# Three box filters and a Fourier block in one program: VectorE's sums, residuals and root in another order, a root of eleven operations, two mixes swapped, GELU ahead of the square

## The chip, the core and the metric

The program runs on one core of one Trainium2 chip. The metric is the device time of a run in microseconds, the median of the runs; lower is better. Everything is computed in float32.

## The reference, cut to what matters

The input is `x` of shape (4, 64, 128, 128): four images with 64 channels. Four layers follow each other. Layers 0, 2 and 3 are box filters with a batch norm on either side; the change does not touch them. Layer 1 is a stack of four identical blocks, and that is where the change lies:

```python
def _block(x, ...):                       # four times, each with its own weights
    residual = x
    xn = _ln(transpose(x), ln1w, ln1b)    # layer norm over the 64 channels: mean, variance, rsqrt
    xf = rfft2(xn)
    o1 = relu(complex_mix(xf, w1) + b1)   # first mix: 64x64 complex, per frequency
    o2 = complex_mix(o1, w2) + b2         # second mix
    o2 = o2 * mask                        # zero where both |re| and |im| are at most 0.01
    x = residual + irfft2(o2)
    xp2 = _ln(transpose(x), ln2w, ln2b)   # second layer norm
    return x + gelu(xp2 @ mw1 + mb1) @ mw2 + mb2
```

Each layer norm needs, for each pixel, the sum and the sum of squares over the channels and then 1/sqrt(variance + 1e-5). The last is what the text calls the root.

## The kernel before, in words

The four images times four blocks make 16 passes through layer 1 (`RUNS`, numbered n = 0 to 15). The function `afno_layers` writes them as a pipeline by hand: while the MLP of pass n runs over 16 blocks of eight rows, the Fourier part of pass n+1 runs in the same stretch. A pass is cut into 16 periods q = 0 to 15, one for each block of rows, and each period into four steps s = 0 to 3; `parts` says which piece of the Fourier part lies in which step: the second half of the inverse transform of pass n in the periods 0, 1 and 4, the forward transform of n+1 in 4 and 5, the mixes (`spectrum`) from 5 to 10, the backward transform in 11, and the first half of the inverse transform in 12 and 13. Every engine walks through the same loop over n, q and s and issues its own share in the order in which the Python code of that engine stands; semaphores tie the engines together. There is no scheduler: the order of the lines is the order on the engine.

What each engine does in a period, with the lines of the profile:

- **TensorE (PE)** turns the previous delta back (`turn_back`, L1765 into the PSUM tile `result`), turns the next normalised block (`turn`, L1759, from `y2`), multiplies with the MLP's weights (`mlp_up` L1739, `mlp_down` L1750 into `result`), and its part of the Fourier transform (inverse L1667 and L1671, forward L1685, spectrum L1696, L1705 and L1714, backward L1729). `mlp_down(i)` writes the same PSUM tile that the residual of block i-1 is read from, so it waits for that residual.
- **VectorE (DVE)** adds the residual (`residual`, L1433), adds the inverse transform's output (`inverse`, L1371, L1372, L1376), takes the sums for the layer norms (`sum_up`: L1452 for the sum, L1455 for the sum of squares), and runs the root (`root`, lines L986 to L1006): twelve small operations on at most 128 x 64 elements that depend on each other one by one. The root of a set of four blocks starts a chain of POOL's.
- **GpSimd (POOL)** finishes the inverse transform (L1263), folds the rows for the forward transform (`fold`, L1298 and L1300), and multiplies with the root: `normalise` (L1275) makes `y2` for PE's turn, `next_y` (L1287) makes the next pass's rows. The first `normalise` after a root and `next_y` wait for that root; the rest only follow in POOL's order.
- **ScalarE (ACT)** takes the squares (`square`, L1593), the GELU (`gelu`, L1559), the copy of the turned block (L1565), the delta for `turn_back` (`mlp_delta`, L1572) and other evictions.
- **SyncE (SP)** loads and stores rows.

The change edits the loops of VectorE, ScalarE and TensorE at the periods q = 1, 2, 10, 13, 14 and 15, and the function `root_step`. Before, VectorE runs the root of the periods 1 and 2 in one piece at q = 1, s = 2, ahead of that period's inverse; and at q = 13 all four sums of two strips follow the inverse, so the residual of q = 14 stands behind them, and the root behind the residual.

## Time and profile before

| | us |
|---|---|
| Three runs: median (lowest to highest) | 3559.46 (3558.67 to 3560.19) |
| The profiled execution: its own time / its span | 3561.85 / 3560.0 |
| Busy in the span: PE / PE's weight loads / DVE / ACT / POOL | 3248.4 / 1965.7 / 2393.6 / 2205.7 / 1649.7 |
| Mean granted TensorE clock | 0.963 of full |

The profile is that of one execution. Its span runs from the first to the last instruction. A gap in square brackets behind a row of the timeline is the idle time of that engine just before the row, and the name behind the arrow is what ended it. Layer 1 fills the stretch from about 190 us to 3170 us; one undisturbed pass of the pipeline takes 174.5 us of it.

### The profile page before, as it was taken

What the parts mean: (1) busy time and instruction counts of PE and PEld (TensorE: products, weight loads), DVE (VectorE), ACT (ScalarE), POOL (GpSimd) and SP (SyncE); (2) the same over time, 40 slices, a digit from 0 to 9 for tenths busy, and PEclk for the clock granted to TensorE, in tenths of its full rate; (3) what the DMA queues carried; (4) which work ended last, traced back from release to release, by engine and by line L of the source; (5) the groups of instructions that cost most, each with busy time, mean ns of one, the idle gap of its engine ahead of it and who ended that gap; (6) DMA issues with size and microseconds to landing.
All of it is one profiled execution on the core that took longest, in us unless ns stands there. A gap on an engine that the chain in (4) does not pass through costs nothing. (4 is left out here: it accounts for less than half of the span.)

```text
span 3560.0 us, 52776 instructions
## 1 busy us (share of the span) xinstructions
PE 3248.4 (91%) x18285; PEld 1965.7 (55%) x18285; DVE 2393.6 (67%) x4148; ACT 2205.7 (62%) x3477; POOL 1649.7 (46%) x1389
## 2 busy tenths in 40 slices
PE   6946699999999999998999999999999999979689
PEld 2735464647474646464647464646474747334257
DVE  4956666767676676766667667676767665536677
ACT  3954466666666666666666666666656565646468
POOL 4435545464646454545454645455454543210242
PEclk7967899999999999999999999999999999999889
DMA  9850001010101011313120101111111111356898
GB/s 324 275 187 24 30 31 62 34 65 31 66 31 66 31 66 37 118 48 137 48 89 31 66 31 65 37 60 44 57 42 54 42 54 42 147 188 190 262 303 239
DMA packets 250279, 334.08 MB, mean 94 GB/s; under 512 B 22304, under 2 KB 195616, under 8 KB 242608
## 3 DMA queue, kind: packets, MB, share of 16 engines
q1 hardware_dynamic: 241664, 315.29, 26.3%
q0 software_dynamic: 7904, 15.57, 1.6%
q8 instruction: 144, 2.36, 0.3%
q14 instruction: 103, 0.84, 0.1%
q10 hardware_dynamic: 464, 0.02, 0.0%
HBM read 188.06 MB, written 142.74 MB: 93 GB/s over the span
## 5 line engine op out<-in xcount | busy, mean ns | idle before, releaser
L1559 ACT ACTIVATE images<-a_wide,a_up_b 128x1024 f32<-128x1024 f32 x512 | 569.8, 1113 | 247.2 <-PE a_wide L1739 245.8
L1739 PE MATMUL a_wide<-images 64*128 64x512 f32 x2048 | 579.2, 641 | 23.8 <-ACT images L1559 23.1
L1317 POOL TENSOR_TENSOR images<-a_o,a_mag 128x256 f32<-128x256 f32 (+1 forms) x512 | 360.6, 731 | 378.3 <-DVE a_mag L1422 378.3
L1750 PE MATMUL a_result<-images 128*64 128x512 f32 x2048 | 499.0, 607 | 34.8 <-DVE images L1433 34.8
L1275 POOL TENSOR_TENSOR images<-images,a_stat 128x512 f32<-128x512 f32 x256 | 268.6, 1050 | 545.7 <-DVEq L1469 527.0
L1402 DVE TENSOR_TENSOR a_o<-a_bank,a_mix_b 128x512 f32<-128x512 f32 (+1 forms) x272 | 180.9, 665 | 249.6 <-PE a_bank L1714 246.7
L1705 PEld LDWEIGHTS a_bank<-a_dft_h,a_g 128*128 128x128 f32 x2080 | 273.5, 192 | 129.9 <-issue 129.9
L1433 DVE TENSOR_TENSOR images<-a_result,images 128x512 f32<-128x512 f32 x256 | 175.6, 686 | 224.8 <-PE a_result L1765 224.6
L1750 PEld LDWEIGHTS a_result<-images 128*64 128x64 f32 x2048 | 128.6, 136 | 355.6 <-issue 339.9
L1739 PEld LDWEIGHTS a_wide<-images 64*128 64x128 f32 x2048 | 156.7, 185 | 287.8 <-issue 258.0
L1455 DVE TENSOR_REDUCE a_stat<-a_sq 128x16 f32<-128x1024 f32 x240 | 290.7, 1211 | 10.5 <-ACT a_sq L1593 8.6
L1696 PE MATMUL a_bank<-a_xf,a_mix_fold 128*128 128x512 f32 (+1 forms) x544 | 286.4, 608 | 5.8 <-ACT a_xf L1546 5.8
L1685 PE MATMUL a_bank<-dft_w,images 128*128 128x128 f32 x2048 | 246.2, 279 | 48.4 <-POOL images L1300 46.2
L1263 POOL TENSOR_TENSOR images<-images,a_odd 128x512 f32<-128x512 f32 (+1 forms) x128 | 161.6, 1263 | 270.1 <-DVE images L1372 260.8
L1572 ACT ACTIVATE images<-a_result,a_down_b 128x512 f32<-128x512 f32 x256 | 175.8, 687 | 176.6 <-PE a_result L1750 176.1
L1452 DVE TENSOR_REDUCE a_stat<-images 128x16 f32<-128x1024 f32 x232 | 281.5, 1213 | 4.8
L1685 PEld LDWEIGHTS a_bank<-dft_w,images 128*128 128x128 f32 x2048 | 235.4, 193 | 84.2 <-POOL images L1300 46.3
L1705 PE MATMUL a_bank<-a_dft_h,a_g 128*128 128x128 f32 x2080 | 278.3, 276 | 1.8 <-DVE a_g L1395 1.8
L1593 ACT ACTIVATE a_sq<-images 128x1024 f32<-128x1024 f32 x216 | 227.3, 1052 | 68.8 <-DVE a_stat L1455 43.0
L1729 PE MATMUL a_bank<-a_dft_hi,images 128*128 128x128 f32 x2048 | 235.4, 277 | 8.9 <-POOL images L1317 8.9
L1729 PEld LDWEIGHTS a_bank<-a_dft_hi,images 128*128 128x128 f32 x2048 | 232.3, 194 | 12.8 <-POOL images L1317 12.8
L1520 ACT ACTIVATE a_g<-a_bank 64x252 f32<-64x252 f32 (+3 forms) x512 | 166.6, 374 | 77.5 <-PE a_bank L1685 58.2
(206 smaller groups left out, 6119.7 us busy)
## 6 DMA issues: line engine op xcount, KB each, us to landing
rows<-images SPq DMA_DIRECT2D x112, 512.0 KB, 2.6
images<-rows SPq DMA_DIRECT2D x105, 512.0 KB, 3.7
box_xc<-in_x SPq DMA_DIRECT2D x16, 1024.0 KB, 16.7
box_x<-in_x SPq DMA_DIRECT2D x64, 256.0 KB, 4.3
turned<-box_o SPq DMA_DIRECT2D x64, 256.0 KB, 3.6
images<-turned SPq DMA_DIRECT2D x16, 1024.0 KB, 11.8
planes<-box_work SPq DMA_DIRECT2D x64, 256.0 KB, 3.7
box_xc<-planes SPq DMA_DIRECT2D x16, 1024.0 KB, 19.2
```

The costliest lines, as they stand in the source:

```text
L1275: G.tensor_tensor(rows(y2[:, i % 2]), x[:, row:row + HB], r[:, :, None].broadcast_to([P, HB, C]), ALU.mult).then_inc(s_y2, 1)
L1317: ins = G.tensor_tensor(y[n % 2][:, :, to].rearrange("p c k -> p k c"), o2[:, j % 3, lo:4, r], mask[:, lo:4], ALU.mult)
L1452: V.tensor_reduce(to, strip, AX.X, ALU.add)
L1455: V.tensor_reduce(to, squares_of(r, kind, u), AX.X, ALU.add).then_inc(s_sq_read, 1)
L1559: A(hidden[:, i % 2, j], wide[:], ACT.Gelu, bias=up_b2[:, l, j:j + 1]).then_inc(s_hid, 1)
L1593: A(squares_of(r, kind, u), strip, ACT.Square).then_inc(s_sq, 1)
L1685: mm = M(bank[i % 4][:, c * P:(c + 1) * P], y[n % 2][:, 4 * i + c, :], dft_w[:], start=True, stop=True)
L1696: M(bank[2][:, 0:cols], mix1_fold[:, l], xf[:, 0:cols], start=True, stop=True).then_inc(s_mix1, 1)
L1705: mm = M(bank[0][:, k * P:(k + 1) * P], g[:, first_kw(t) + k].rearrange("p r c -> p (r c)"), dft_h[:], start=True, stop=True)
L1729: mm = M(bank[i % 4][:, c * P:(c + 1) * P], y[n % 2][:, 4 * i + c, :], dft_hi[:], start=True, stop=True)
L1739: mm = M(wide[:, half * BANK:(half + 1) * BANK], up_fold[cs, l, j * P:(j + 1) * P], yc[cs, i % 2], start=True, stop=True)
L1750: mm = M(result[half * C:(half + 1) * C, :], down[:, l, j, :], hidden[:, i % 2, j, half * BANK:(half + 1) * BANK], start=j == 0, stop=j == ...
```

## The change

It does five things; no matrix product, sum, residual or DMA is added or taken away.

- The root takes eleven operations: the shift and the subtraction of its first guess become one multiplication and addition.
- At q = 1 VectorE issues the inverse first, then the first five operations of the root; the other six follow the residual at q = 2.
- At q = 13 the sum of the strip of q = 12 goes ahead of the inverse; the sum of squares of the strip of q = 13 moves behind the residual of q = 14, and the one of q = 14 behind the residual of q = 15.
- TensorE issues the last but one second mix ahead of the last first mix.
- ScalarE issues the second GELU of q = 14 ahead of that period's square, and in passes that do not stage a new image also at q = 15.

```diff
-ROOT_STEPS = 12
+ROOT_STEPS = 11
...
-        ins = V.tensor_scalar(r.bitcast(I32), v.bitcast(I32), 1, None, ALU.logical_shift_right)
-    elif j == 4:
-        ins = V.tensor_scalar(r.bitcast(I32), r.bitcast(I32), -1.0, float(RSQRT_GUESS), ALU.mult, ALU.add)
+        ins = V.tensor_scalar(r.bitcast(I32), v.bitcast(I32), -0.5, float(RSQRT_GUESS), ALU.mult, ALU.add)
...
                     if q not in CLOSED and 0 <= Q - 2 < BLOCKS * RUNS:
                         residual(Q - 2)
-                    if q == 14 and FIRST_ROOT <= r < END_ROOT:
-                        root(r, range(ROOT_STEPS))
-                    strips = (strips_at(n, 12)[1:] if q == 13 else []) + strips_at(n, q)[:1]
+                    if q == 2 and FIRST_ROOT <= SETS * n < END_ROOT:
+                        root(SETS * n, range(ROOT_STEPS // 2, ROOT_STEPS))
+                    if q == 13:
+                        for strip in strips_at(n, 12)[1:]:
+                            sum_up(*strip, 0)
+                    if q == 14:
+                        for strip in strips_at(n, 13)[:1]:
+                            sum_up(*strip, 1)
+                        if rooted:
+                            root(r, range(ROOT_STEPS))
+                    if q == 15:
+                        for strip in strips_at(n, 14)[:1]:
+                            sum_up(*strip, 1)
+                    strips = strips_at(n, q)[:1]
...
                         parts(n, q, s, inverse, forward, spectrum, backward)
+                        if q == 13 and s == 1:
+                            for strip in strips_at(n, 12)[1:]:
+                                sum_up(*strip, 1)
                         if s == late:
                             for strip in strips:
                                 sum_up(*strip, 0)
-                                if q not in CLOSED:
+                                if q not in CLOSED and q not in (13, 14):
                                     sum_up(*strip, 1)
...
-                            if q == 1 and s == (2 if q in CLOSED else 1):
-                                root(r, range(ROOT_STEPS))
-                            if (q, s) in ((5, 3), (9, 2)):
+                            if (q, s) in ((1, 3), (5, 3), (9, 2)):
                                 root(r, range(ROOT_STEPS // 2))
...
-                    if q != 12 and not (q % 4 == 3 and fresh(n)):
+                    if q not in (12, 14, 15) and not (q % 4 == 3 and fresh(n)):
                         for strip in strips_at(n, q):
                             square(*strip)
                     parts(n, q, 1, inverse, forward, spectrum, backward)
                     if q not in CLOSED and 0 <= Q < BLOCKS * RUNS:
                         gelu(Q, 1)
-                    if q == 12:
+                    if q in (12, 14) or q == 15 and not fresh(n):
                         for strip in strips_at(n, q)[:1]:
                             square(*strip)
...
+                    if t == N_CHUNK:
+                        second_mix(t - 2)
+                    if 0 <= t - 1 < N_CHUNK:
+                        first_mix(t - 1)
```

On VectorE at the periods 1 and 2 of a pass, before: the end of the root (its last three operations of twelve, L996 to L1006), the inverse of q = 1 (L1371 to L1376), the residual of q = 2 (L1433), then a sum.

```order
L996 TENSOR_TENSOR a_stat<-a_stat 128x64
L1004 SCALAR_TENSOR_TENSOR a_stat<-a_stat 128x64
L1006 SCALAR_TENSOR_TENSOR a_stat<-a_stat 128x64
L1371 TENSOR_TENSOR images<-a_bank,images 128x512
L1372 TENSOR_TENSOR images<-a_bank,images 128x512
L1376 TENSOR_TENSOR images<-a_bank,images 128x512
L1433 TENSOR_TENSOR images<-a_result,images 128x512
L1452 TENSOR_REDUCE a_stat<-images 128x16
```

And with the change (line numbers of the new file: the inverse is L1369 to L1374, the residual L1431, the sums L1450 and L1453):

```order
L1453 TENSOR_REDUCE a_stat<-a_sq 128x16
L1369 TENSOR_TENSOR images<-a_bank,images 128x512
L1370 TENSOR_TENSOR images<-a_bank,images 128x512
L1374 TENSOR_TENSOR images<-a_bank,images 128x512
L986 SCALAR_TENSOR_TENSOR a_stat<-a_stat 128x64
L988 SCALAR_TENSOR_TENSOR a_stat<-a_stat 128x64
L990 TENSOR_SCALAR a_stat<-a_stat 128x64
L992 TENSOR_SCALAR a_stat<-a_stat 128x64
L994 TENSOR_TENSOR a_stat<-a_stat 128x64
L1431 TENSOR_TENSOR images<-a_result,images 128x512
L996 TENSOR_TENSOR a_stat<-a_stat 128x64
L998 SCALAR_TENSOR_TENSOR a_stat<-a_stat 128x64
```

The inverse moved ahead of the whole root, and seven of the root's twelve operations no longer stand ahead of the residual: five do.

On VectorE from the period 13 to the start of the root at 14, before: the residual of q = 13, the inverse, the sums of two strips (`a_mag` holds the squares of the first), the residual of q = 14, the root.

```order
L1433 TENSOR_TENSOR images<-a_result,images 128x512
L1371 TENSOR_TENSOR images<-a_bank,images 128x512
L1372 TENSOR_TENSOR images<-a_bank,images 128x512
L1376 TENSOR_TENSOR images<-a_bank,images 128x512
L1452 TENSOR_REDUCE a_stat<-images 128x16
L1455 TENSOR_REDUCE a_stat<-a_mag 128x16
L1452 TENSOR_REDUCE a_stat<-images 128x16
L1455 TENSOR_REDUCE a_stat<-a_sq 128x16
L1433 TENSOR_TENSOR images<-a_result,images 128x512
L986 SCALAR_TENSOR_TENSOR a_stat<-a_stat 128x64
```

And with the change:

```order
L1431 TENSOR_TENSOR images<-a_result,images 128x512
L1450 TENSOR_REDUCE a_stat<-images 128x16
L1369 TENSOR_TENSOR images<-a_bank,images 128x512
L1370 TENSOR_TENSOR images<-a_bank,images 128x512
L1374 TENSOR_TENSOR images<-a_bank,images 128x512
L1453 TENSOR_REDUCE a_stat<-a_mag 128x16
L1450 TENSOR_REDUCE a_stat<-images 128x16
L1431 TENSOR_TENSOR images<-a_result,images 128x512
L1453 TENSOR_REDUCE a_stat<-a_sq 128x16
L986 SCALAR_TENSOR_TENSOR a_stat<-a_stat 128x64
```

Two of the four sums no longer stand between the inverse and the residual of q = 14: one went ahead of the inverse, one behind the residual.

On TensorE at the period 10, before: the last first mix (L1696), the last but one second mix (L1714 from `a_odd`), the turns, the last second mix (L1714 from `a_o`).

```order
L1739 MATMUL a_wide<-images 128x512 x2
L1696 MATMUL a_bank<-a_xf,a_mix_fold 128x512
L1714 MATMUL a_bank<-a_mix,a_odd 128x128 x4
L1765 MATMUL a_result<-ident,images 128x128 x4
L1759 MATMUL a_turned<-ident,images 128x128 x4
L1714 MATMUL a_bank<-a_mix,a_o 128x128 x4
```

And with the change (L1757, L1783 and L1777 are the old L1739, L1765 and L1759; the first mix is L1707):

```order
L1757 MATMUL a_wide<-images 128x512 x2
L1714 MATMUL a_bank<-a_mix,a_odd 128x128 x4
L1707 MATMUL a_bank<-a_xf,a_mix_fold 128x512
L1783 MATMUL a_result<-ident,images 128x128 x4
L1777 MATMUL a_turned<-ident,images 128x128 x4
L1714 MATMUL a_bank<-a_mix,a_o 128x128 x4
```

The second mix went ahead of the first mix; nothing else moved there.

## Rows read from the trace of the kernel before

**Rows 1.** Stretches: us, busy PE, PEld, DVE, ACT, POOL, PEclk, DMA, GB/s.
```profile
2183.30:2357.80 174.50, 169.62 (x974) 102.84 (x972) 122.14 (x215) 110.15 (x163) 91.19 (x77) 1.00 0.14 49
...
1851.20:1854.60 3.40, 3.40 (x10) 1.06 (x8) 1.74 (x2) 1.34 (x2) 3.40 (x3) 0.50 0.02 5
```

**Rows 2.** Groups of PE by line, whole span: busy, mean ns | idle before.
```profile
L1750 PE MATMUL a_result<-images 128*64 128x512 f32 x2048 | 499.0, 607 | 34.8 <-DVE images L1433 34.8
...
L1759 PE MATMUL a_turned<-ident,images 128*128 128x128 f32 x1024 | 156.2, 275 | 32.3 <-POOL images L1275 32.3
```

**Rows 3.** Timeline of PE, pass 10, periods 14 and 15: start, us.
```profile
2345.31 0.66 PE L1765 MATMUL a_result<-ident,images 128*128 128x128 f32 x4
...
2348.70 1.94 PE L1750 MATMUL a_result<-images 128*64 128x512 f32 x8 [0.88 <-DVE images L1433]
...
2352.68 0.66 PE L1759 MATMUL a_turned<-ident,images 128*128 128x128 f32 x4 [0.40 <-POOL images L1275]
...
2354.68 1.94 PE L1750 MATMUL a_result<-images 128*64 128x512 f32 x8 [0.29 <-DVE images L1433]
2356.78 1.13 PE L1739 MATMUL a_wide<-images 64*128 64x512 f32 x4 [0.16 <-ACT images L1559]
```

**Rows 4.** Timeline of PE, pass 10, periods 2 to 4.
```profile
2200.20 1.94 PE L1750 MATMUL a_result<-images 128*64 128x512 f32 x8 [0.93 <-DVE images L1433]
...
2204.50 1.13 PE L1739 MATMUL a_wide<-images 64*128 64x512 f32 x4 [0.28 <-ACT images L1559]
2205.56 1.94 PE L1750 MATMUL a_result<-images 128*64 128x512 f32 x8
...
2210.24 0.66 PE L1759 MATMUL a_turned<-ident,images 128*128 128x128 f32 x4 [1.10 <-POOL images L1275]
```

**Rows 5.** Timeline of PE, pass 10, period 11.
```profile
2309.58 0.60 PE L1729 MATMUL a_bank<-a_dft_hi,images 128*128 128x128 f32 x3 [0.28 <-POOL images L1317]
```

**Rows 6.** Timeline of DVE, pass 10, periods 13 and 14.
```profile
2341.43 0.69 DVE L1371 TENSOR_TENSOR images<-a_bank,images 128x512 f32<-128x512 f32 x1 [1.09 <-PE a_bank L1671]
...
2345.62 1.21 DVE L1452 TENSOR_REDUCE a_stat<-images 128x16 f32<-128x1024 f32 x1
...
2347.87 0.68 DVE L1433 TENSOR_TENSOR images<-a_result,images 128x512 f32<-128x512 f32 x1
2348.47 0.22 DVE L986 SCALAR_TENSOR_TENSOR a_stat<-a_stat 128x64 f32<-128x64 f32 x1
```

**Rows 7.** Timeline of POOL, pass 10, period 14.
```profile
2351.59 1.04 POOL L1275 TENSOR_TENSOR images<-images,a_stat 128x512 f32<-128x512 f32 x1 [7.44 <-DVEq L1469]
```

**Rows 8.** Timeline of ACT, pass 10, period 15.
```profile
2354.57 1.06 ACT L1593 ACTIVATE a_sq<-images 128x1024 f32<-128x1024 f32 x1 [0.60 <-DVE images L1433]
```

**Rows 9.** Timeline of DVE, pass 10, periods 1 and 2.
```profile
2193.99 0.54 DVE L986 SCALAR_TENSOR_TENSOR a_stat<-a_stat 128x64 f32<-128x64 f32 x1
...
2197.44 0.69 DVE L1371 TENSOR_TENSOR images<-a_bank,images 128x512 f32<-128x512 f32 x1
...
2199.37 0.68 DVE L1433 TENSOR_TENSOR images<-a_result,images 128x512 f32<-128x512 f32 x1
```

**Rows 10.** Timeline of POOL, pass 10, periods 1 and 2.
```profile
2198.88 1.27 POOL L1263 TENSOR_TENSOR images<-images,a_odd 128x512 f32<-128x512 f32 x1 [4.42 <-DVE images L1372]
2200.10 2.40 POOL L1300 TENSOR_TENSOR images<-images,a_upper 128x1024 f32<-128x1024 f32 x1
2202.44 1.06 POOL L1275 TENSOR_TENSOR images<-images,a_stat 128x512 f32<-128x512 f32 x1
```

**Rows 11.** Timeline of DVE in the start-up: a root beside folds.
```profile
252.71 2.23 DVE L990 TENSOR_SCALAR a_stat<-a_stat 128x32 f32<-128x32 f32 x1
254.97 2.24 DVE L992 TENSOR_SCALAR a_stat<-a_stat 128x32 int32<-128x32 int32 x1
```

**Rows 12.** Timeline of POOL in the same stretch: the second of two folds.
```profile
254.85 2.32 POOL L1300 TENSOR_TENSOR images<-images,a_upper 128x960 f32<-128x960 f32 x1
```

**Rows 13.** Timeline of PE, pass 8, period 2.
```profile
1850.83 3.38 PE L1750 MATMUL a_result<-images 128*64 128x512 f32 x8 [1.97 <-DVE images L1433]
```

More of the change, by code:

```diff
@@ L991, in root_step @@
     elif j == 3:
-        ins = V.tensor_scalar(r.bitcast(I32), v.bitcast(I32), 1, None, ALU.logical_shift_right)
-    elif j == 4:
-        ins = V.tensor_scalar(r.bitcast(I32), r.bitcast(I32), -1.0, float(RSQRT_GUESS), ALU.mult, ALU.add)
-    elif j in (5, 9):
+        ins = V.tensor_scalar(r.bitcast(I32), v.bitcast(I32), -0.5, float(RSQRT_GUESS), ALU.mult, ALU.add)
+    elif j in (4, 8):
         ins = V.tensor_tensor(total, r, r, ALU.mult)
+    elif j == 5:
+        ins = V.tensor_tensor(total, total, v, ALU.mult)
     elif j == 6:
-        ins = V.tensor_tensor(total, total, v, ALU.mult)
+        ins = V.scalar_tensor_tensor(out=total, in0=total, scalar=-10.0 / 3.0, in1=total, op0=ALU.add, op1=ALU.mult)
     elif j == 7:
-        ins = V.scalar_tensor_tensor(out=total, in0=total, scalar=-10.0 / 3.0, in1=total, op0=ALU.add, op1=ALU.mult)
-    elif j == 8:
         ins = V.scalar_tensor_tensor(out=r, in0=total, scalar=5.0, in1=r, op0=ALU.add, op1=ALU.mult)
-    elif j == 10:
+    elif j == 9:
         ins = V.scalar_tensor_tensor(out=total, in0=total, scalar=-0.5 * CUBIC ** 3, in1=v, op0=ALU.mult, op1=ALU.mult)
@@ L1476, in _ @@
                         fold_weights()
+                    rooted = FIRST_ROOT <= r < END_ROOT
                     if q in CLOSED and 0 <= Q - 2 < BLOCKS * RUNS:
@@ L1696, in spectrum, with second_mix @@
                         M(bank[2][:, 0:cols], mix1_fold[:, l], xf[:, 0:cols], start=True, stop=True).then_inc(s_mix1, 1)
+                    def second_mix(j):
+                        pe.wait_ge(s_o1, before + j + 1)
+                        if j >= 1:
+                            pe.wait_ge(s_o2, before + j)
+                        for k in range(chunk(j)):
+                            mm = M(bank[3][:, k * P:(k + 1) * P], o1_of(j)[:, k * P:(k + 1) * P], mix2[:, l],
+                                   start=True, stop=True)
+                        mm.then_inc(s_mix2, 1)
+                    if t == N_CHUNK:
+                        second_mix(t - 2)
+                    if 0 <= t - 1 < N_CHUNK:
+                        first_mix(t - 1)
                     if t < N_CHUNK:
@@ L1707, in spectrum @@
                         mm.then_inc(s_fh, 1)
-                    j = t - 2
-                    if 0 <= j < N_CHUNK:
-                        pe.wait_ge(s_o1, before + j + 1)
-                        if j >= 1:
-                            pe.wait_ge(s_o2, before + j)
-                        for k in range(chunk(j)):
-                            mm = M(bank[3][:, k * P:(k + 1) * P], o1_of(j)[:, k * P:(k + 1) * P], mix2[:, l],
-                                   start=True, stop=True)
-                        mm.then_inc(s_mix2, 1)
+                    if t >= 2 and t != N_CHUNK:
+                        second_mix(t - 2)
                     if t == 8:
```

5 lines of the change are left out of this document (2 added, 3 removed).

## The prediction

> **What bounds the kernel now.** I read the stretches first, then PE's groups by line, then the timelines of PE, VectorE, POOL and ScalarE in one pass. In pass 10 PE is busy 169.6 of 174.5 us at the full clock [rows 1]; the other engines are at most 70% busy. So PE's work sets the length of a pass, and an edit on another engine gains only what it takes out of PE's waits. Two of those waits are large in the groups by line: `mlp_down` (L1750) waits 34.8 us for the residual, and the turn (L1759) waits 32.3 us for POOL's multiplication by the root [rows 2]. Both come once per pass at fixed places, so I work in pass 10 and multiply. Its waits are, at q = 14 and 15: 0.88 for the residual, 0.40 for POOL, 0.29 for the residual, 0.16 for the GELU [rows 3]; at q = 2: 0.93 for the residual; at q = 4: 1.10 for POOL [rows 4]; at q = 11: 0.28 for POOL's masked product [rows 5]. Together 4.04 us. A shown gap understates its wait a little: L1750 follows L1739 after 1.06 us where nothing waits, although L1739 lasts 1.13 [rows 4]; so 0.07 more goes with each, 4.5 us in all. Over 15 passes that is an upper limit of about 68 us.
>
> **Periods 13 to 15.** Before, VectorE is free for the third of four sums at 2345.62, runs two more to 2347.87 and only then adds the residual [rows 6], whose input PE had ready at 2345.31 + 0.66 = 2345.97 [rows 3]. With the change two sums stand there instead of four. The one put ahead of the inverse takes (2347.87 - 2345.62) / 2 = 1.13 us and falls into the 1.09 us in which VectorE waits for PE anyway [rows 6], so it costs nothing; without that cover it would cost 1.13 us of VectorE's time, and the residual would still come 0.7 us earlier. The residual starts at about 2346.0, 1.85 us earlier, and PE's wait of 0.88 + 0.07 = **0.95** goes. The root follows: residual 0.6, one sum 1.13, a handover of 0.1 give 2347.85 instead of 2348.47; from there to POOL's L1275 it is 2351.59 - 2348.47 = 3.12 us for twelve operations [rows 6, 7], 0.26 each, and eleven save 0.26. So POOL starts 0.6 + 0.2 = 0.8 us earlier. PE, 0.95 earlier, waits for it a little longer than before, and what is left is 0.8. At q = 15 the residual no longer stands behind a sum of squares: 0.29 + 0.07 goes. ScalarE's square of 1.06 us [rows 8] now follows the GELU, so the GELU that PE waits for comes earlier, and 0.16 + 0.07 goes. The square then delays the delta that the next turn back needs; by my count it ends 0.05 to 0.1 us before PE wants it, so this term is full or lost by a tenth. Sum for q = 13 to 15: **-1.4 us** a pass.
>
> **Periods 1 to 4.** This is the disputed part. Before, the root runs from 2193.99 to the inverse at 2197.44, and the residual follows at 2199.37, 1.93 us for three additions [rows 9]. During the root POOL sits idle: its L1263 waits 4.42 us for the inverse's second addition and starts at 2198.88, then the fold L1300 and L1275 follow without a gap [rows 10]. With the change the inverse comes first, 2193.99 to 2195.9, and POOL starts as much ahead of the additions' end as before, 2199.37 - 2198.88 = 0.49, so at 2195.4; the fold runs from 2195.4 + 1.22 = 2196.6 to 2199.0. Now the first five operations of the root run beside L1263 and the fold. What that costs is seen in the start-up: an operation of the root that takes 0.18 to 0.26 us alone took 2.23 and 2.24 us beside POOL's fold [rows 11]; the second was issued at 254.97, just behind the start of a fold at 254.85, and ended when that fold did [rows 12]. So one operation of the root gets in between two POOL instructions, and the next waits for the whole of the second. The Trainium skill (SBUF — State Buffer, Who interferes with whom) says the same: one port pair is shared by VectorE and GpSimd and held for a whole instruction, by VectorE when both its inputs lie in SBUF or it runs in a two-port mode, never by a reduction. By that rule, taken strictly with the fold already queued, the very first operation would wait for the fold's end too, and a pass would gain 0.25 us less; the rows show one getting through, and I keep to them.
>
> So L986 ends with L1263 at 2196.6, L988 with the fold at 2199.0, and three more take 0.75: the residual comes at 2199.75, **0.38 later** than before although seven operations of the root moved behind it. PE's wait at q = 2 grows by 0.38. Without the block it would come at 2195.9 + 5 x 0.26 = 2197.2, two us earlier than before, and the wait of 1.0 would go; these are the ends of this term, and the rows on the block are nearest. The second half, six operations of 0.26 behind a residual of 0.6, with POOL idle and waiting for them, ends at 2201.9, and L1275 starts at 2202.0 instead of 2202.44. From there to the turn at q = 4 POOL runs without a gap, so the turn comes 0.44 earlier, which leaves PE **-0.45 us** over the stretch, the 0.38 included.
>
> **Period 10.** The swapped mixes and the shorter first half of that root let VectorE's last masks come 0.2 to 0.5 us earlier, and with them the masked product that PE waits for at q = 11. Between 0 and 0.28 + 0.07, and a tenth at the mix itself, I take **-0.4**. The first mix, 0.9 later, feeds ScalarE just in time.
>
> **Sum.** A pass gains 1.4 + 0.45 + 0.4 = 2.25 us. That holds for eleven passes, 0 to 5 and 9 to 13: 24.8. In passes 6 to 8 and 14 other waits stand in some of these places (ScalarE's copies of the next image, a pass without the waits at q = 14), and I count them at half, 4 x 1.1 = 4.5. In the start-up, by the code, four roots lie on the path to the first matrix product, 4 x 0.26 = 1. Together 30 us. The profiled execution took 3561.85 us, 2.4 over the median; the sum taken from it gives 3531.5, and against the median **3529 us**.
>
> **Rivals.**
> - *No block.* The root's first half runs at 0.26 an operation beside POOL. For it: in pass 10 the root's first operation took only 0.54 [rows 9]. Against it: rows 11 and 12. Then q = 2 gains 1.0 and q = 4 the whole 1.17: 4.0 a pass, 44 over eleven passes, 10 in the other four, 1 at the start: 3504. Chance 0.12.
> - *ScalarE's tail.* The square between GELU and delta holds PE's turn back at q = 15 and 0. One whole square each would cost 2 x 1.06 = 2.1 a pass and leave almost nothing: 3555. Against it stands the room of 0.05 to 0.1 us, which a small delay can use up, but not a whole square. Chance 0.12, mostly at 3540 to 3550.
> - *TensorE's clock (slower).* In pass 8 the wait at q = 2 was 1.97 us, and the eight L1750 behind it took 3.38 instead of 1.94 [rows 4, 13]; the granted clock there was 0.50, the 1.2 GHz level, after an idle stretch [rows 1]. The forecast lengthens that wait to about 1.3 us in each pass. If it fell each time and stayed low to the turn at q = 4, the 8.3 us of work from 2200.20 to 2210.24 - 1.10 - 0.66 would take 1.74 times as long, 6.1 more. It decides from about 2.5 us of loss a pass on: what the rest gains, and what the wait at q = 4 still covers. 6.1 gives +3.5 a pass: about 3593. Against it: 1.10 us of idle at q = 4 lowers nothing, and in pass 8 the low level lasted 3.4 us, a loss of 1.7. Chance 0.06.
>
> **How the numbers follow.** The forecast has 0.70: 3519 to 3541, with tenths at the tail and at q = 11 and the strict rule at its bounds. The range has to leave out no more than 0.2: from 3502, which takes in *no block*, to 3546, which takes in the better half of *ScalarE's tail*. About 0.2%, 7 us, is what a measurement can tell from no change. Faster: the forecast, *no block* and some of the tail, 0.87; same: the rest of the tail, 0.07; slower: the clock, 0.06.
>
> **What would show it.** In a pass of the changed kernel L1750 at q = 14 and 15 should follow without a gap; POOL's L1275 at q = 14 should start about 0.8 us sooner behind PE's turn back; at q = 1 one operation of the root should last about 0.7 and the next about 2.3 us, beside L1263 and the fold; PE should wait some 1.3 us at q = 2 and at most 0.5 at q = 4; a pass should take some 172.2 us. It is wrong if the root at q = 1 shows no long operation (then more is gained), or if L1765 gets a wait for the delta or the clock of a plain pass falls below 1.

## The result, and the profile after

The changed kernel takes **3528.61 us** (median of six runs, 3526.71 to 3532.79) where the kernel before takes 3559.65 in the same comparison: a ratio of 0.9916, 95% interval 0.9902 to 0.9929, so 0.7 to 1.0% faster. The profiled execution took 3532.79 us with a span of 3531.0, against 3561.85 and 3560.0 before. One of the six runs of before was disturbed (5032.62 us): it is in that median, which would be 3559.46 without it, and not in the ratio.

Where the 29.0 us between the two spans come from, by the start of PE's first turn back in each pass (pass 0 has none yet and is taken from its second turn):

| stretch | before | after | difference | predicted |
|---|---|---|---|---|
| start of the span to pass 0 | 418.35 | 412.79 | -5.6 | -1 |
| pass 0 | 176.70 | 175.67 | -1.0 | -2.25 |
| passes 1 to 5 and 9 to 13 | 1745.44 | 1722.53 | -22.9 | -22.5 |
| passes 6 to 8 | 540.92 | 540.98 | +0.1 | -3.4 |
| pass 14 | 172.70 | 171.98 | -0.7 | -1.1 |
| pass 15 to the end | 505.9 | 507.1 | +1.2 | 0 |

A plain pass went from 174.5 to 172.2 us, as forecast to the tenth; the sum is right too, but two of its other terms missed and cancelled each other, which was luck. The 1.2 us at the end are no more than single executions differ there: 505.1 to 507.0 over the ten kernels of this document.

The stretches of the changed kernel, pass 10 and passes 7 and 8 together (us, busy PE, PEld, DVE, ACT, POOL, PEclk, DMA, GB/s):

```profile
2162.90:2335.10 172.20, 169.39 (x974) 102.61 (x972) 123.37 (x212) 109.89 (x163) 91.19 (x77) 1.00 0.15 50
1629.70:1990.80 361.10, 345.99 (x1945) 207.38 (x1945) 246.63 (x423) 235.83 (x336) 180.40 (x153) 0.98 0.20 73
```

and passes 7 and 8 of the kernel before:

```profile
1648.90:2008.80 359.90, 343.06 (x1945) 206.61 (x1945) 243.48 (x431) 236.06 (x336) 180.92 (x153) 0.99 0.20 74
```

PE does the same 974 operations in pass 10 [rows 1], so the 2.3 us are waits. PE's groups by line, whole span (L1768 is the old L1750, L1777 the old L1759):

```profile
L1768 PE MATMUL a_result<-images 128*64 128x512 f32 x2048 | 499.4, 608 | 23.2 <-ACT images L1570 12.3 <-DVE images L1431 10.9
...
L1777 PE MATMUL a_turned<-ident,images 128*128 128x128 f32 x1024 | 156.8, 276 | 23.4 <-POOL images L1273 23.4
```

34.8 us of waiting at `mlp_down` became 23.2, and 32.3 at the turn became 23.4 [rows 2]. The view puts half of the 23.2 down to ScalarE's GELU; that is a wait for two semaphores where the GELU ends 0.15 us behind the residual, and the experiment `residual_first` shows which of them counts.

**Periods 14 and 15.** PE's timeline in pass 10:

```profile
2324.03 0.66 PE L1783 MATMUL a_result<-ident,images 128*128 128x128 f32 x4
...
2326.46 1.94 PE L1768 MATMUL a_result<-images 128*64 128x512 f32 x8
...
2330.56 0.66 PE L1777 MATMUL a_turned<-ident,images 128*128 128x128 f32 x4 [0.52 <-POOL images L1273]
...
2332.21 1.94 PE L1768 MATMUL a_result<-images 128*64 128x512 f32 x8
2334.07 1.13 PE L1757 MATMUL a_wide<-images 64*128 64x512 f32 x4
2335.13 0.66 PE L1783 MATMUL a_result<-ident,images 128*128 128x128 f32 x4
```

The gaps of 0.88, 0.29 and 0.16 [rows 3] are gone; the one for POOL grew from 0.40 to 0.52. The last row, the turn back that waits for the delta, has no gap, so ScalarE's square behind the GELU held nothing up. POOL's first multiplication by the root:

```profile
2329.47 1.04 POOL L1273 TENSOR_TENSOR images<-images,a_stat 128x512 f32<-128x512 f32 x1 [6.61 <-DVEq L1467]
```

It starts 5.44 us behind the turn back, against 2351.59 - 2345.31 = 6.28 before [rows 3, 7]: 0.84 sooner.

**Periods 1 to 4.** VectorE at q = 1 and 2:

```profile
2173.51 0.68 DVE L1369 TENSOR_TENSOR images<-a_bank,images 128x512 f32<-128x512 f32 x1
...
2175.43 0.85 DVE L986 SCALAR_TENSOR_TENSOR a_stat<-a_stat 128x64 f32<-128x64 f32 x1
2176.32 2.29 DVE L988 SCALAR_TENSOR_TENSOR a_stat<-a_stat 128x64 f32<-128x64 f32 x1
2178.64 0.20 DVE L990 TENSOR_SCALAR a_stat<-a_stat 128x64 f32<-128x64 f32 x1
...
2179.25 0.68 DVE L1431 TENSOR_TENSOR images<-a_result,images 128x512 f32<-128x512 f32 x1
```

and POOL beside it:

```profile
2174.93 1.27 POOL L1261 TENSOR_TENSOR images<-images,a_odd 128x512 f32<-128x512 f32 x1 [0.35 <-DVE images L1370]
2176.16 2.37 POOL L1298 TENSOR_TENSOR images<-images,a_upper 128x1024 f32<-128x1024 f32 x1
2181.50 1.04 POOL L1273 TENSOR_TENSOR images<-images,a_stat 128x512 f32<-128x512 f32 x1 [2.97 <-DVEq L1467]
```

This is the block as predicted: L986 ends 0.08 behind L1261's end (2176.28 and 2176.20), L988 0.08 behind the fold's (2178.61 and 2178.53); the next takes 0.20 again. PE's waits there:

```profile
2180.08 1.94 PE L1768 MATMUL a_result<-images 128*64 128x512 f32 x8 [1.18 <-ACT images L1570]
...
2189.30 0.66 PE L1777 MATMUL a_turned<-ident,images 128*128 128x128 f32 x4 [0.27 <-POOL images L1273]
```

0.93 became 1.18 and 1.10 became 0.27 [rows 4]. Around q = 11 the product that waited for the masked one follows without a gap (L1747, the old L1729), where it had 0.28 [rows 5]:

```profile
2288.30 3.95 PE L1747 MATMUL a_bank<-a_dft_hi,images 128*128 128x128 f32 x33
```

**Passes 0, 7 and 8.** PE in pass 8, q = 0 and q = 2, and two stretches of it:

```profile
1814.31 0.66 PE L1783 MATMUL a_result<-ident,images 128*128 128x128 f32 x4 [1.91 <-ACT images L1583]
...
1834.56 2.98 PE L1768 MATMUL a_result<-images 128*64 128x512 f32 x8 [2.54 <-DVE images L1431]
```

```profile
1814.90:1818.20 3.30, 3.30 (x9) 1.72 (x7) 2.65 (x4) 1.91 (x3) 0.46 (x1) 0.50 0.86 319
1835.40:1838.70 3.30, 3.30 (x10) 0.80 (x6) 2.76 (x4) 0.69 (x1) 2.72 (x2) 0.50 0.02 5
```

The wait at q = 2, which was 1.97 [rows 13], is 2.54 now, and behind that and behind the wait of 1.91 at q = 0 the granted clock is 0.50, the 1.2 GHz level. The wait at q = 0 is one for ScalarE's delta, which stands there behind the copy of the next image and a square; the kernel before had it too, 1.58 long, without a fall of the clock behind it:

```profile
1832.84 0.66 PE L1765 MATMUL a_result<-ident,images 128*128 128x128 f32 x4 [1.58 <-ACT images L1572]
```

Pass 7 shows the same, and in pass 0 the clock fell behind a wait of 2.07:

```profile
432.26 3.56 PE L1768 MATMUL a_result<-images 128*64 128x512 f32 x8 [2.07 <-DVE images L1431]
```

Two such stretches stood in the passes of before, five stand in those of after. They took back what these passes gained: by the rows for passes 7 and 8 above, PE's waits there fell by 1.7 us (359.90 - 343.06 = 16.8 to 361.10 - 345.99 = 15.1), and its busy time grew by 2.9.

**The start-up.** PE from the first product of the first spectrum (L1705, later L1730) to the 130th, in the kernel before and in the changed one:

```profile
313.30:360.30 47.00, 44.48 (x272) 35.31 (x273) 30.28 (x58) 25.36 (x37) 26.74 (x29) 0.93 0.06 23
313.30:357.70 44.40, 41.70 (x271) 33.56 (x272) 30.23 (x57) 25.27 (x37) 26.73 (x29) 1.00 0.06 25
```

Some 2.5 of the 5.6 us lie here, and they go with the granted clock, 0.93 against 1.00. Of the kernels below, `mix_as_before` and `q1_as_before` take 47.0 us here at 0.93 too and the other six 44.5 at 1.00. So this part follows none of the change's parts; it is put down to the single execution, as each kernel was profiled once, and that is not shown further. Three other stretches do follow the change. From PE's first product with the weights (L1652, later L1663) to the first forward product it is 58.0 us with twelve operations in the root and 57.0 to 57.2 with eleven. From the 130th product to the first of the inverse it is 32.0 to 32.4 with the old order of the mixes, and with the new one 29.8 to 30.1 in five kernels and 31.3 in one. From there to the first turn it is 21.9 before and 21.1 after. The rest goes 0.3 one way and 1.1 the other.

### The profile page after: what moved, and what is told of

It reads as the page before. It is cut to its first block and busy times, and to the rows that moved or that the text cites. A ratio compares the mean times of both kernels' runs of the same rounds, so it can differ in the third digit from the quotient of the medians.

```text
span 3531.0 us, 52706 instructions
## 1 busy us (share of the span) xinstructions
PE 3248.8 (92%) x18285; PEld 1963.4 (56%) x18285; DVE 2410.7 (68%) x4078; ACT 2202.9 (62%) x3477; POOL 1649.7 (47%) x1389
## 5 line engine op out<-in xcount | busy, mean ns | idle before, releaser
L1757 PE MATMUL a_wide<-images 64*128 64x512 f32 x2048 | 580.5, 643 | 22.0 <-ACT images L1570 21.3
L1768 PE MATMUL a_result<-images 128*64 128x512 f32 x2048 | 499.4, 608 | 23.2 <-ACT images L1570 12.3
L1730 PEld LDWEIGHTS a_bank<-a_dft_h,a_g 128*128 128x128 f32 x2080 | 272.4, 191 | 129.4 <-issue 129.4
L1768 PEld LDWEIGHTS a_result<-images 128*64 128x64 f32 x2048 | 126.0, 136 | 344.1 <-issue 308.7
L1757 PEld LDWEIGHTS a_wide<-images 64*128 64x128 f32 x2048 | 156.6, 185 | 287.2 <-issue 257.4
L1431 DVE TENSOR_TENSOR images<-a_result,images 128x512 f32<-128x512 f32 x256 | 175.5, 686 | 194.6 <-PE a_result L1783 194.4
L1453 DVE TENSOR_REDUCE a_stat<-a_sq 128x16 f32<-128x1024 f32 x240 | 290.7, 1211 | 19.9 <-ACT a_sq L1604 19.5
L1696 PE MATMUL a_bank<-dft_w,images 128*128 128x128 f32 x2048 | 247.3, 279 | 47.5 <-POOL images L1298 45.4
L1707 PE MATMUL a_bank<-a_xf,a_mix_fold 128*128 128x512 f32 (+1 forms) x544 | 283.2, 602 | 6.0 <-ACT a_xf L1557 6.0
L1450 DVE TENSOR_REDUCE a_stat<-images 128x16 f32<-128x1024 f32 x232 | 281.5, 1213 | 6.7
L1696 PEld LDWEIGHTS a_bank<-dft_w,images 128*128 128x128 f32 x2048 | 236.5, 194 | 83.2 <-POOL images L1298 45.5
L1730 PE MATMUL a_bank<-a_dft_h,a_g 128*128 128x128 f32 x2080 | 277.3, 275 | 2.2 <-DVE a_g L1393 2.2
L1261 POOL TENSOR_TENSOR images<-images,a_odd 128x512 f32<-128x512 f32 (+1 forms) x128 | 161.2, 1260 | 217.6 <-DVE images L1370 210.1
L1747 PE MATMUL a_bank<-a_dft_hi,images 128*128 128x128 f32 x2048 | 234.5, 277 | 4.6 <-POOL images L1315 4.6
L1747 PEld LDWEIGHTS a_bank<-a_dft_hi,images 128*128 128x128 f32 x2048 | 231.6, 193 | 8.0 <-POOL images L1315 8.0
```

The costliest lines, as they stand in the source:

```text
L1450: V.tensor_reduce(to, strip, AX.X, ALU.add)
L1453: V.tensor_reduce(to, squares_of(r, kind, u), AX.X, ALU.add).then_inc(s_sq_read, 1)
L1696: mm = M(bank[i % 4][:, c * P:(c + 1) * P], y[n % 2][:, 4 * i + c, :], dft_w[:], start=True, stop=True)
L1707: M(bank[2][:, 0:cols], mix1_fold[:, l], xf[:, 0:cols], start=True, stop=True).then_inc(s_mix1, 1)
L1730: mm = M(bank[0][:, k * P:(k + 1) * P], g[:, first_kw(t) + k].rearrange("p r c -> p (r c)"), dft_h[:], start=True, stop=True)
L1747: mm = M(bank[i % 4][:, c * P:(c + 1) * P], y[n % 2][:, 4 * i + c, :], dft_hi[:], start=True, stop=True)
```

## The experiments

Eight kernels ran, each beside the kernel before, whose median was 3558.84 us in the first comparison (`q1_as_before` to `square_first`) and 3559.86 in the second. "After" is the changed kernel; a plain pass is the median of the ten passes 1 to 5 and 9 to 13, by their starts in the profile.

| kernel | median us | ratio, 95% interval | plain pass |
|---|---|---|---|
| after | 3528.61 | 0.9916, 0.9902 to 0.9929 | 172.2 |
| `q1_as_before` | 3534.72 | 0.9933, 0.9919 to 0.9946 | 173.1 |
| `residual_first` | 3516.81 | 0.9882, 0.9867 to 0.9897 | 171.8 |
| `psum_root` | 3499.85 | 0.9835, 0.9822 to 0.9848 | 170.6 |
| `square_first` | 3533.02 | 0.9933, 0.9920 to 0.9947 | 172.8 |
| `tail_only` | 3548.47 | 0.9970, 0.9959 to 0.9981 | 173.9 |
| `q1_only` | 3557.95 | 0.9995, 0.9986 to 1.0004 | 174.1 |
| `mix_as_before` | 3537.81 | 0.9934, 0.9920 to 0.9947 | 172.6 |
| `psum_sum_first` | 3493.73 | 0.9814, 0.9801 to 0.9828 | 170.1 |

### Does the block hold the residual up: `residual_first`

```diff
                     if q == 2 and FIRST_ROOT <= SETS * n < END_ROOT:
-                        root(SETS * n, range(ROOT_STEPS // 2, ROOT_STEPS))
+                        root(SETS * n, range(1, ROOT_STEPS))
...
-                            if (q, s) in ((1, 3), (5, 3), (9, 2)):
+                            if (q, s) == (1, 3):
+                                root(r, range(1))
+                            if (q, s) in ((5, 3), (9, 2)):
```

> The changed kernel, with the residual of q = 2 put behind the first operation of the root instead of behind the fifth. Theory (the second operation waits for the whole of POOL's fold, and holds up the residual only because the residual is queued behind it; the residual itself, which reads PSUM, runs beside the fold at 0.7 us): the residual ends about 1.9 us earlier in the pass, PE's gap at q = 2 (1.18 us) goes; the operation of 2.3 us stays but is shorter, as it starts later and still ends with the fold; ten operations end about 0.5 us sooner, since the residual's time no longer stands behind the fold. POOL's first multiplication by the root comes 0.4 to 0.5 us earlier, and PE, 1.2 earlier, now waits for POOL at q = 4 instead: about 1.1 us. A plain pass gains only those 0.4 to 0.5 us: 171.7 to 171.8; in passes 0, 7 and 8, where the wait at q = 2 was over 2 us, up to 2 more each. Total 3516 to 3524. Rival (POOL's fold holds up VectorE as a whole, the residual too): nothing changes, 3527 to 3530.

Measured: 3516.81 us, a plain pass of 171.8. VectorE, then POOL, then PE in pass 10:

```profile
2164.85 0.69 DVE L1431 TENSOR_TENSOR images<-a_result,images 128x512 f32<-128x512 f32 x1 [0.71 <-PE a_result L1785]
2165.46 1.02 DVE L988 SCALAR_TENSOR_TENSOR a_stat<-a_stat 128x64 f32<-128x64 f32 x1
```

```profile
2164.03 2.37 POOL L1298 TENSOR_TENSOR images<-images,a_upper 128x1024 f32<-128x1024 f32 x1
```

```profile
2166.59 1.94 PE L1770 MATMUL a_result<-images 128*64 128x512 f32 x8
...
2176.68 0.66 PE L1779 MATMUL a_turned<-ident,images 128*128 128x128 f32 x4 [0.88 <-POOL images L1273]
```

The residual runs in 0.69 in the middle of the fold (2164.03 to 2166.40), while L988 behind it still ends with that fold. PE's gap at q = 2 is gone, so it was the residual that ended it in the changed kernel, not the GELU that the view names. About half of it reappears at q = 4 as a wait for POOL, 0.88 instead of 0.27 (about 1.1 was expected). The theory stands; the rival falls.

### Does it depend on where the operands lie: `psum_root`

```diff
+    total, total_sq, t_copy, r = (view(q) for q in range(4))
+    v, u, t = (scratch(q) for q in range(3))
...
+        ins = V.tensor_tensor(u, v, r, ALU.mult)
+        ins = V.tensor_tensor(t, u, r, ALU.mult)
+        ins = V.tensor_tensor(t_copy, u, r, ALU.mult)
+        ins = V.scalar_tensor_tensor(out=t, in0=t, scalar=-10.0 / 3.0, in1=t_copy, op0=ALU.add, op1=ALU.mult)
...
-                        root(SETS * n, range(ROOT_STEPS // 2, ROOT_STEPS))
+                        root(SETS * n, range(5, PSUM_STEPS), True)
```

(`view` is the tile `stat` in SBUF, `scratch` a piece of `bank[0]` in PSUM, which is free from q = 1 to q = 4.)

> The changed kernel in its order, but the root of periods 1 and 2 keeps its intermediate values in a PSUM bank that is free there, so that each of its operations but the first reads one operand from PSUM; that takes a twelfth operation (a second copy of one product). Theory (an operation is held up by POOL's fold only where all its operands lie in SBUF): no operation but the first lasts over 0.5 us; the four behind it end about 1.2 us after it instead of 3.0; the residual of q = 2 no longer delays PE (gap 0 instead of 1.18), and the root ends about 1.5 us earlier, POOL's first multiplication by it about 1.5 us sooner, so the gap of 0.27 at q = 4 doesn't grow by more than 0.1. A plain pass takes 170.8 to 171.2 us; over thirteen passes 16 to 20 us, and a little more in passes 0, 7 and 8: 3502 to 3514 us. Rival A (any small operation waits for the fold, wherever its operands lie): the second operation lasts 2.3 us as now, and one operation more costs 0.26 a pass: 3529 to 3534. Rival B (operands in PSUM make each operation so slow, 0.4 us and more, that nothing is won): 3520 to 3528.

Measured: 3499.85 us, below the expected 3502 to 3514; a plain pass of 170.6. VectorE, then POOL, then PE in pass 10:

```profile
2150.13 0.86 DVE L1021 SCALAR_TENSOR_TENSOR a_bank<-a_stat 128x64 f32<-128x64 f32 x1
2151.02 0.23 DVE L1023 SCALAR_TENSOR_TENSOR a_bank<-a_stat,a_bank 128x64 f32<-128x64 f32 x1
...
2151.95 0.68 DVE L1470 TENSOR_TENSOR images<-a_result,images 128x512 f32<-128x512 f32 x1
```

```profile
2150.85 2.37 POOL L1337 TENSOR_TENSOR images<-images,a_upper 128x1024 f32<-128x1024 f32 x1
```

```profile
2153.39 1.94 PE L1814 MATMUL a_result<-images 128*64 128x512 f32 x8
...
2162.28 0.66 PE L1823 MATMUL a_turned<-ident,images 128*128 128x128 f32 x4
```

The same operation that took 2.29 us beside the fold takes 0.23 with one operand in PSUM, beside a fold of the same 2.37. The first one, whose operands all lie in SBUF, still takes 0.86. Both of PE's gaps, at q = 2 and q = 4, are gone, in spite of one operation more. The Trainium skill (SBUF — State Buffer, Who interferes with whom) says that a VectorE instruction with at most one SBUF input, outside the two-port modes, does not contend with GpSimd; these rows agree. Beyond the expectation came passes 7 and 8, where the wait at q = 2 fell from 2.5 to 0.55 us and the clock fell once instead of four times:

```profile
1614.20:1967.00 352.80, 341.16 (x1944) 206.50 (x1944) 242.67 (x425) 236.04 (x336) 180.46 (x153) 1.00 0.20 75
```

These two passes take 352.8 us against 361.1 in the changed kernel, 8.3 of the 35.8 us between the two profiled spans (the medians lie 28.8 apart): 4.8 less of busy time, 3.5 less of waits.

### Undoing the split in the changed kernel: `q1_as_before`

```diff
-                    if q == 2 and FIRST_ROOT <= SETS * n < END_ROOT:
-                        root(SETS * n, range(ROOT_STEPS // 2, ROOT_STEPS))
...
-                            if (q, s) in ((1, 3), (5, 3), (9, 2)):
+                            if (q, s) == (1, 2):
+                                root(r, range(ROOT_STEPS))
+                            if (q, s) in ((5, 3), (9, 2)):
```

> The changed kernel, with the root of periods 1 and 2 put back in one piece ahead of the inverse (still eleven operations). Theory (the split brings little, because its first half stands beside POOL's fold): the residual of q = 2 comes only by one operation, 0.26 us, earlier than in the kernel before, so PE waits about 0.7 us at q = 2 and about 1.1 at q = 4, against 1.18 and 0.27 now: a plain pass takes 172.4 to 172.5 us instead of 172.2, and L986 lasts at most 0.6 us with no operation of this root over 1 us. Over some twelve passes +2 to +3; in passes 0, 7 and 8 the shorter wait at q = 2 may spare a stretch of 3.4 us at the 1.2 GHz level, up to 1.7 us each. Total 3526 to 3532 us, against 3528.6 for the changed kernel. Rival (putting the inverse first is where the gain of periods 1 to 4 comes from): a pass loses a microsecond or more, 3540 us or above.

Measured: 3534.72 us and 173.1 a pass, outside the expectation of 3526 to 3532 and 172.4 to 172.5, and short of the rival. The undoing cost 0.9 a pass where the two waits of before, less one operation, make 0.93 - 0.26 + 1.10 - 1.18 - 0.27 = 0.3; in pass 11 PE waits 1.34 us at q = 2 and 1.09 at q = 4. VectorE, then POOL in that pass:

```profile
2342.69 0.69 DVE L1369 TENSOR_TENSOR images<-a_bank,images 128x512 f32<-128x512 f32 x1 [1.83 <-DMA images<-rows]
...
2347.71 1.08 DVE L986 SCALAR_TENSOR_TENSOR a_stat<-a_stat 128x64 f32<-128x64 f32 x1
```

```profile
2344.12 1.28 POOL L1261 TENSOR_TENSOR images<-images,a_odd 128x512 f32<-128x512 f32 x1 [4.12 <-DVE images L1370]
...
2347.67 1.05 POOL L1273 TENSOR_TENSOR images<-images,a_stat 128x512 f32<-128x512 f32 x1
```

The root's first operation waits for the whole of POOL's multiplication of q = 1; in the kernel before it waited for its second half only, 0.54 [rows 9]. That multiplication follows POOL's first one behind the root of q = 14 at a steady distance, 16.4 us here and 16.3 in the kernel before, although POOL idles for 4 us in between (L1261). The delay travels by way of a load: `reload` on SyncE waits until POOL's last multiplication behind that root is done (L1285 ends at 2339.0, the load is issued at 2339.08 and lands 3.5 us later), VectorE's inverse of q = 0 (L1369) waits for these rows, and POOL for the inverse. The tail gave PE 1.4 us and POOL 0.84, so POOL's multiplication now lies 0.6 later against PE and VectorE, and with the root ahead of the inverse everything behind it, the residual of q = 2 too, comes that much later. From this came a new theory: the parts are not independent, and the tail's gain is kept only because the split takes the root out of POOL's way.

### Each part alone on the kernel before: `tail_only` and `q1_only`

`tail_only` has the new order of the periods 13 to 15 on VectorE and ScalarE, `q1_only` the split:

```diff
+                    if q == 2 and FIRST_ROOT <= SETS * n < END_ROOT:
+                        root(SETS * n, range(5, ROOT_STEPS))
...
-                            if q == 1 and s == (2 if q in CLOSED else 1):
-                                root(r, range(ROOT_STEPS))
+                            if (q, s) == (1, 3):
+                                root(r, range(5))
```

> The kernel before, with only the change's order of the periods 13 to 15 (the two sums, the squares behind the GELU); root of twelve operations, in one piece ahead of the inverse at q = 1, mixes as before. Theory (the parts are not independent): at q = 13 to 15 a pass gains about 1.2 us (0.95 for the residual of q = 14, 0.36 and 0.23 at q = 15, less 0.35 by which PE then waits longer for POOL). But POOL's work behind that root runs without a gap up to its multiplication of q = 1, and comes only 0.6 us earlier, so that multiplication now lies 0.5 to 0.6 us later against the sums that the root of q = 1 follows; the root's first operation waits for its end (about 1.1 us instead of 0.54), and the root, the inverse and the residual of q = 2 behind it come that much later: PE's gap at q = 2 grows from 0.93 to about 1.5. A plain pass keeps 0.6 to 0.7 us: 173.8 to 173.9, in all 3549 to 3553 us. Rival (the terms add up as in the prediction): 173.3 us a pass, 3543 to 3546.

> The kernel before, with only the root of periods 1 and 2 split: inverse first, five of its twelve operations, the residual of q = 2, seven more. Theory: as in the prediction's term, with one operation more: the second operation lasts about 2.3 us beside the fold, the residual comes 0.3 to 0.4 later, POOL's multiplication by the root 0.1 to 0.2 earlier; PE's gap at q = 2 grows to 1.3, the one at q = 4 falls to 0.5 to 0.6. A plain pass gains 0.1 to 0.3 us: 174.2 to 174.4; passes 0, 7 and 8 may lose up to 1.7 us each to the clock. 3554 to 3560 us in all. Rival (the split alone brings the 0.9 us a pass that its undoing cost in the changed kernel): 173.6, 3545 to 3549.

Measured: `tail_only` 3548.47 us, half a microsecond below the expected 3549 to 3553, and 173.9 a pass, on the theory and not on the sum of terms (173.3). Its VectorE, POOL and PE in pass 10:

```profile
2181.03 1.07 DVE L986 SCALAR_TENSOR_TENSOR a_stat<-a_stat 128x64 f32<-128x64 f32 x1
```

```profile
2180.97 1.05 POOL L1275 TENSOR_TENSOR images<-images,a_stat 128x512 f32<-128x512 f32 x1
```

```profile
2187.77 1.94 PE L1763 MATMUL a_result<-images 128*64 128x512 f32 x8 [1.46 <-DVE images L1433]
```

The gap at q = 2 grew from 0.93 to 1.46, as expected to the tenth. The expectation is wrong in one link: POOL's work does not run without a gap up to its multiplication of q = 1, it idles 4.00 us at q = 0 here too and gets its delay by the load. `q1_only`: 174.1 a pass, 0.1 better than expected, but 3557.95 us in all, no measurable change (the interval holds 1): in its profiled execution the ten plain passes gained 2.9 us together, and passes 0, 7 and 8 gave 1.8 back, 0.4 to 0.9 each. PE in its pass 10:

```profile
2197.81 1.94 PE L1752 MATMUL a_result<-images 128*64 128x512 f32 x8 [1.14 <-DVE images L1433]
...
2207.26 0.66 PE L1761 MATMUL a_turned<-ident,images 128*128 128x128 f32 x4 [0.50 <-POOL images L1275]
```

So alone the tail is worth 0.6 a pass and the split 0.4; undone in the changed kernel, the split is worth 0.9. At q = 13 to 15 the tail gains 1.2 alone too (from the turn back of q = 14 to that of the next q = 0 it is 12.53 us before, 11.34 in `tail_only`, 11.10 with the change); at q = 2 it loses 0.5 of that. The shorter root ran in no kernel by itself. `tail_only` and `q1_as_before` differ only by it and by the order of the mixes, and of the 0.8 us a pass between them the mixes make 0.4 (next section), so by this difference it is worth some 0.4; PE's wait for POOL at q = 15 is 0.75 in the one and 0.53 in the other.

### The squares and the mixes: `square_first` and `mix_as_before`

```diff
-                    if q not in (12, 14, 15) and not (q % 4 == 3 and fresh(n)):
+                    if q != 12 and not (q % 4 == 3 and fresh(n)):
...
-                    if q in (12, 14) or q == 15 and not fresh(n):
+                    if q == 12:
```

> The changed kernel, with ScalarE's squares of q = 14 and 15 put back ahead of the second GELU. Theory: at q = 15 PE waits 0.2 us again for the GELU; at q = 14 the square has to wait for the sum of squares of q = 13, which the change moved behind the residual, and holds the GELU up by about 1 us, of which PE sees 0 to 0.5. Together +0.2 to +0.7 a pass: 3531 to 3538. Rival (ScalarE's tail: the square between GELU and delta holds up the turn back): undoing it makes the kernel faster, below 3526.

Measured: 3533.02 us, 0.6 more a pass; ScalarE, then PE, at q = 14 of pass 10:

```profile
2324.29 1.06 ACT L1604 ACTIVATE a_sq<-images 128x1024 f32<-128x1024 f32 x1 [0.88 <-DVE a_stat L1453]
```

```profile
2326.50 1.13 PE L1757 MATMUL a_wide<-images 64*128 64x512 f32 x4 [0.44 <-ACT images L1570]
```

The square waits for VectorE to have read the squares of q = 13 (there is one buffer), which the change moved behind the residual; ahead of the GELU it passes that wait on to PE. At q = 15 PE waits 0.46 for the GELU, where 0.2 was expected. So this reordering is needed by the one on VectorE, and ScalarE's tail, the rival, falls.

`mix_as_before` puts the old order of `spectrum` back:

```diff
-                    if t == N_CHUNK:
-                        second_mix(t - 2)
...
-                    if t >= 2 and t != N_CHUNK:
+                    if t >= 2:
                         second_mix(t - 2)
```

> The changed kernel, with TensorE's last first mix put back ahead of the last but one second mix. Theory: the second mix comes 0.5 us later again, and with it VectorE's last masks and POOL's masked product; of the 0.35 us that PE no longer waits around q = 11, 0.1 to 0.35 come back: 172.3 to 172.5 us a pass, 3530 to 3533 in all. Of the start-up the same: of the 4.5 us that the first pass of the Fourier part gained, more than 1 is lost if the mixes' order made it. Rival (the shorter root alone cleared q = 11, and the swap does nothing): 3527 to 3530, no gap of 0.2 or more at q = 11.

Measured: 172.6 a pass, a tenth over the expectation, and PE's gap is back in full:

```profile
2292.69 7.52 PE L1740 MATMUL a_bank<-a_dft_hi,images 128*128 128x128 f32 x65 [0.28 <-POOL images L1315]
```

So the shorter root alone does nothing for this gap, and the swap was needed to clear it; whether the swap would have done it beside the root of twelve operations was not run. In the first pass of the Fourier part the stretch of 30.1 us in the start-up is 32.0 again, so the order of the mixes made that part of the start-up's gain. The total, 3537.81, is 5 us over the expectation. The profiled executions lie 5.4 us apart, of which the ten plain passes make 3.7 and the later start of pass 0 1.75 (414.54 against 412.79; in this execution the start-up also has the 2.5 us of lower clock). The medians lie 9.2 apart, as the profiled execution was the slowest of the changed kernel's six; the rest stays open.

### A version that beats both: `psum_sum_first`

```diff
+                    if q == 14:
+                        for strip in strips_at(n, 13)[:1]:
+                            sum_up(*strip, 1)
                     if q not in CLOSED and 0 <= Q - 2 < BLOCKS * RUNS:
                         residual(Q - 2)
...
-                    if q == 14:
-                        for strip in strips_at(n, 13)[:1]:
-                            sum_up(*strip, 1)
-                        if rooted:
-                            root(r, range(ROOT_STEPS))
+                    if q == 14 and rooted:
+                        root(r, range(ROOT_STEPS))
```

> The kernel with the root of periods 1 and 2 in PSUM, and besides the sum of squares of q = 13 put back ahead of the residual of q = 14, so that of the change's two moves there only the first is left. Theory: with one sum ahead of the inverse, VectorE is free at about the time at which PE's turn back is done, so a sum of 1.13 us ahead of the residual makes that only 0.75 later, and PE, which needs it 1.7 us after the residual now starts, doesn't notice; VectorE's idle 0.31 ahead of the residual goes, the root starts 0.4 to 0.5 us earlier, POOL's first multiplication by it too, and PE's gap of 0.52 at q = 15 falls to about 0.1. A plain pass takes 170.1 to 170.2 us instead of 170.5, 3493 to 3497 in all, against 3499.85. Rival (the residual is late again, as in the kernel before): a gap at q = 14, and 3500 us or more.

Measured: 3493.73 us, 1.9% under the kernel before and the fastest here; 170.1 a pass. VectorE's residual, then PE in pass 10:

```profile
2295.12 0.68 DVE L1470 TENSOR_TENSOR images<-a_result,images 128x512 f32<-128x512 f32 x1
```

```profile
2296.12 1.94 PE L1814 MATMUL a_result<-images 128*64 128x512 f32 x8
...
2299.71 0.66 PE L1823 MATMUL a_turned<-ident,images 128*128 128x128 f32 x4
```

The residual, 0.75 behind what it could be, still ends 0.3 before PE asks for it, and POOL is no longer late at q = 15. Of the change's two moves at q = 14, the sum ahead of the inverse was the one needed.

## Why the prediction was right, and where not

- **Periods 13 to 15: -1.4 a pass.** Right, term by term: 0.95 for the residual, 0.12 given back at POOL (0.15 predicted), the waits at q = 15 gone, the delta in time. The price was right only in the company of the split: alone the same order gives 0.6 (`tail_only`). The prediction took each group of periods by itself; that POOL's delay of q = 14 comes back at q = 1, by way of the load of rows and the inverse, and that a late POOL blocks the root there, it did not see.
- **Periods 1 to 4: -0.45.** Right in mechanism and size: gap at q = 2 up by 0.25 (0.38 predicted), at q = 4 down by 0.83 (0.83 predicted), so -0.58. The rows of the start-up [rows 11, 12] carried over: one operation gets in between two of POOL's instructions, the next waits for the second. The rule of the Trainium skill (SBUF — State Buffer, Who interferes with whom), in the strict reading weighed in the prediction, would have held the first operation to the fold's end; it ended 0.08 behind L1261. `psum_root` shows the cause, and what the rival *no block* would have been worth: 1.6 a pass.
- **Period 10: -0.4.** Right in size (0.28 + 0.07 at q = 11, and a little at the mix); the shorter first half of the root, which the prediction names beside the swap, clears nothing there by itself (`mix_as_before`).
- **Passes 0, 6 to 8 and 14.** Pass 0 counted in full and the others "at half" failed: 6.7 us predicted, 1.7 measured. The rival *TensorE's clock* was placed in the plain passes, where the wait of 1.18 us at q = 2 lowered nothing; it happened where that wait had been 1.5 to 2 us before, in passes 0, 7 and 8, and in the last two also at q = 0, where PE, earlier now, waits 1.91 instead of 1.58 for ScalarE. The growth of the wait at q = 2 was predicted, the loss was not counted. `psum_root`, where that wait is 0.55, takes 8 us less for passes 7 and 8.
- **The start-up: -1.** 5.6 were measured. The shorter root gave its 0.8 up to the first forward product, as predicted. The order of the mixes gave some 2 us between the first spectrum and the first inverse, and 0.8 went between there and the first turn; neither is in the term. Some 2.5 go with the clock of the profiled execution, and 1.1 went the other way.
- So that the total came out, 30 us predicted and 31.0 measured between the medians, is luck in part: two errors of about 5 us have opposite signs; the ten plain passes, 22.9 us of the 29.0 between the spans, are what was understood.

## What to carry to other kernels

A wait that is removed on one engine moves the others against each other, so a term holds only beside the edits it was made with: undo each part of a change in the finished kernel, and put each alone on the old one, before saying what it is worth. Small operations of VectorE that must run beside GpSimd are worth giving one operand in PSUM, where some is free; that brought 1.6 us a pass here, against 2.3 for the whole change. An operation that reads PSUM can also be queued ahead of one that would wait for GpSimd, instead of behind it.

## What was not expected of the hardware

- How much the operand's place decides for additions and multiplications of two operands, at 128x64 and at 128x512: the same step of 128x64 took 2.29 us with its operands in SBUF and 0.23 with one in PSUM, each beside a fold of 2.37 us; and a residual with one operand in PSUM ran in its usual 0.69 in the middle of a fold.
- Reading and writing PSUM made these small operations no slower: 0.22 to 0.23 us against 0.20 to 0.23 in SBUF.
- Whether TensorE's clock falls is not told by the length of a wait alone. In the changed kernel the waits of 1.18 to 1.42 us at q = 2 lowered it in none of the ten plain passes, and waits of 1.91, 2.07, 2.53 and 2.54 each were followed by 3.4 us at the 1.2 GHz level. But in `q1_as_before` one wait of 1.45 in a plain pass was followed by such a stretch, and the like ones of the other nine, 1.19 to 1.38, were not; in `tail_only` ten of 1.41 to 1.69 were not, and in `square_first` one of 2.53 was not either. PE in pass 10 of `q1_as_before`, the eight L1768 at 3.50 instead of 1.94:

```profile
2180.71 3.50 PE L1768 MATMUL a_result<-images 128*64 128x512 f32 x8 [1.45 <-DVE images L1431]
```
